# A tower of attention, a selective scan and routed experts for four images: decays of odd late states in SBUF, and another order of the last image's tail

## What is computed

```
h = prelu(((gamma * (q @ k.T)) @ v) @ Wo + bo)            # retention, gamma is 1024 x 1024
x_conv = silu(x_main @ W_conv + b_conv)                    # 128 channels
dt = softplus(x_conv @ W_dt + b_dt);  B, C = x_conv @ W_bc
for s in range(16):                                        # 16 states of 128 channels
    h_s[t] = exp(dt[t] * A[:, s]) * h_s[t-1] + dt[t] * x_conv[t] * B[t, s]
    y[t] += h_s[t] * C[t, s]
out1 = layernorm(h + (y * silu(x_gate)) @ W_out + b_out)
f = relu(out1 @ Wi.T + bi)
for l in range(2):                                         # 64 tokens share one routed expert of 16
    f = relu(shared_l(f) + expert_l(f) + f)
out = layernorm(out1 + f @ Wo.T + bo)
```

## Time and profile before

| | us |
|---|---|
| median of 3 runs (351.4 to 352.4) | 352.08 |
| the profiled execution's own time | 354.25 |
| its span, first to last instruction | 351.9 |
| busy: PE 280.4, DVE 262.4, POOL 259.5, ACT 191.0 | |
| mean granted TensorE clock, share of full speed | 0.902 |

### The profile page before, as it was taken

One profiled execution on the slowest core, in us unless ns is written; L12 is line 12 of the kernel. 1 busy time (PEld: TensorE's weight loads), 2 busy tenths in 40 slices (PEclk: granted clock), 3 DMA queues, 4 the chain that ended last, 5 costly groups with the idle time before them and its releaser, 6 DMA issues.

```text
span 351.9 us, 4676 instructions
## 1 busy us (share of the span) xinstructions
PE 280.4 (80%) x1426; PEld 160.4 (46%) x1426; DVE 262.4 (75%) x287; ACT 191.0 (54%) x298; POOL 259.5 (74%) x136
## 2 busy tenths in 40 slices
PE   8998838784965889998895999977647846887996
PEld 5423402332453343465632434756434535636664
DVE  2466669989778989987989899879988766249420
ACT  2105823337895243689674337893785843357532
POOL 1027067998999999999999799899978889349300
PEclk9999959998789899999999899987976995588999
DMA  7960596766699997776999877678999999536200
GB/s 234 417 258 0 160 313 225 236 249 257 226 306 304 278 394 270 240 277 193 325 307 374 284 239 235 244 233 278 321 304 313 296 309 340 163 122 177 45 2 15
DMA packets 47128, 85.88 MB, mean 244 GB/s; under 512 B 7936, under 2 KB 24832, under 8 KB 46848
## 3 DMA queue, kind: packets, MB, share of 16 engines
q1 hardware_dynamic: 46704, 84.43, 72.8%
q10 hardware_dynamic: 400, 1.17, 1.1%
HBM read 75.62 MB, written 1.57 MB: 219 GB/s over the span
## 4 chain that ended last, share of the span: by engine, by line
PE 24%; DVE 13%; ACT 9%; DMA 6%; issue 4%; POOL 3%; SPq 2%; DVEq 0%; POOLq 0%; ACTq 0%
DVE h L1331 9%; PE acc_y L661 5%; PE tail L720 4%; DMA c_row<-bc_dram 4%; POOL ub L1191 2%; PE acc_r L614 2%; DMA b_row<-bc_dram 2%; PE work L603 2%; DVE decay L1303 2%; ACT decay L915 1%; PE work L752 1%; POOL hc L1202 1%; PE decay L537 1%; ACT decay_own L915 1%; ACT decay L942 1%
## 5 line engine op out<-in xcount | busy, mean ns | idle before, releaser
L1202 POOL TENSOR_TENSOR hc<-h,c_row 128x1024 f32<-128x1024 f32 (+1 forms) x79 | 154.3, 1961 | 30.0 <-DVE h L1331 24.4
L1191 POOL TENSOR_TENSOR ub<-u,b_row 128x1024 f32<-128x1024 f32 (+1 forms) x49 | 98.1, 2003 | 17.2 <-DVE u L1377 11.6
L661 PEld LDWEIGHTS acc_y<-pack,hc 128*128 128x128 f32 x512 | 63.8, 154 | 48.7 <-issue 34.7
L661 PE MATMUL acc_y<-pack,hc 128*128 128x128 f32 x512 | 78.2, 298 | 9.4 <-ACT y_t L1025 4.9
L915 ACT ACTIVATE decay<-delta,neg_a 128x512 f32<-128x512 f32 (+1 forms) x64 | 51.3, 812 | 62.7 <-DVE h L1331 62.1
L1331 DVE TENSOR_TENSOR_SCAN h<-decay,ub 128x512 f32<-128x512 f32 (+1 forms) x41 | 66.0, 1609 | 12.4 <-POOL ub L1191 6.4
L603 PE MATMUL work<-q,kT 64*128 64x512 f32 x112 | 33.7, 679 | 18.4 <-DVE mixed L1357 14.1
L942 ACT ACTIVATE decay<-u 128x512 f32<-128x512 f32 (+1 forms) x42 | 26.5, 640 | 30.4 <-DVE h L1331 30.2
L1303 DVE TENSOR_TENSOR decay<-decay,b_row 128x512 f32<-128x512 f32 (+1 forms) x40 | 30.8, 769 | 14.4 <-DMA b_row<-bc_dram 8.6
L1357 DVE TENSOR_TENSOR mixed<-gam,work 128x512 f32<-128x512 f32 x56 | 35.5, 676 | 7.9 <-PE work L603 7.1
L614 PE MATMUL acc_r<-mixed,v_sb 128*64 128x512 f32 x128 | 36.9, 657 | 1.1 <-DVE mixed L1357 1.0
(11 more groups left out here) (206 smaller groups left out, 347.0 us busy)
## 6 DMA issues: line engine op xcount, KB each, us to landing
b_row<-bc_dram SPq DMA_DIRECT2D x64, 512.0 KB, 5.3
c_row<-bc_dram SPq DMA_DIRECT2D x64, 512.0 KB, 5.9
group_w<-expert_w SPq DMA_DIRECT2D x48, 128.0 KB, 5.0
gam<-gammaT SPq DMA_DIRECT2D x8, 512.0 KB, 10.6
expert_w<-routed_w SPq DMA_DIRECT2D x1, 2048.0 KB, 18.4
gam<-expert_w SPq DMA_DIRECT2D x16, 128.0 KB, 4.7
x_in<-xT SPq DMA_DIRECT2D x4, 256.0 KB, 9.0
pack<-packed ACTq DMA_DIRECT2D x1, 788.0 KB, 6.7
```

The source lines that it names most:

```text
L661: mm = nc.tensor.matmul(acc_y[:, to:to + P], hc[:, at:at + P], ident, start=(job.state == 0 and c % 4 == 0), stop=(job.state == STATES - 1 ...
L1191: nc.gpsimd.tensor_tensor(ub[:, ring(made, job.halves)], u[:, job.image % 2, tokens(q)], b_row[:, ring(job.at, job.halves)], ALU.mult).the ...
L1202: nc.gpsimd.tensor_tensor(hc[:, here], h[:, here], c_row[:, here], ALU.mult).then_inc(hc_ready, job.halves)
```

## The change

Six edits in one:

1. State 12 of images 0 to 2 joins `VECTOR_JOBS`.
2. `KEPT_JOBS`: the vector jobs, and states 7, 9, 11, 13 and 15 of images 0 to 2, have their decays in decay_own (SBUF). `SLOT_JOBS` are the jobs that use slot: all but these odd states. A scan of an odd late state thus reads decay_own and ub.
3. No scan is cut in two any more (`halved` is gone), and no fill of slot either.
4. decay_own grows to 2T, ub shrinks to 2T.
5. In image 3: one late expert load a step over 16 steps in place of two over 8; one dummy matmul of 256 columns (`keep_warm`) in each half step from 2 to 19.
6. The tail of image 2 goes over half steps 2 to 30 (2 + 8 * m // 5), and the eviction of y on ACT moves from half step 19 to 20.

```diff
 VECTOR_JOBS = [q for q, job in enumerate(JOBS)
-               if job.state in ((0, 4, 8, 10, 14) if job.image not in SPLIT else range(0, STATES, 2))]
+               if job.state in ((0, 4, 8, 10, 12, 14) if job.image not in SPLIT else range(0, STATES, 2))]
+KEPT_JOBS = [q for q, job in enumerate(JOBS)
+             if q in VECTOR_JOBS or job.image not in SPLIT and job.state in (7, 9, 11, 13, 15)]
+SLOT_JOBS = [q for q in range(len(JOBS)) if q in VECTOR_JOBS or q not in KEPT_JOBS]
...
-HALF_ACT = {19: "y", 22: "square1", 23: "log1", 24: "f", 26: "layer1", 28: "layer2", 29: "square2", 30: "log2", 31: "rows"}
+HALF_ACT = {20: "y", 22: "square1", 23: "log1", 24: "f", 26: "layer1", 28: "layer2", 29: "square2", 30: "log2", 31: "rows"}
...
+WARM_FROM, WARM_TO = 2, 20
...
-        ub = sb("ub", [P, 3 * T])
-        decay_own = sb("decay_own", [P, T])
+        ub = sb("ub", [P, 2 * T])
+        decay_own = sb("decay_own", [P, 2 * T])
...
-                steps += [(p - 1, m) for m in range(LAST_STEPS) if 2 + 3 * m // 2 == 2 * n + i]
+                steps += [(p - 1, m) for m in range(LAST_STEPS) if 2 + 8 * m // 5 == 2 * n + i]
...
-        def halved(q):
-
-            return JOBS[q].halves == 2 and JOBS[q].state >= TILES - 1
+        def kept_made(q):
+
+            return sum(JOBS[s].halves for s in KEPT_JOBS if s < q)
+
+        def slot_left(q):
+
+            used = [s for s in SLOT_JOBS if s < q and (JOBS[q].halves == 2 or JOBS[s].halves == 2
+                                                       or JOBS[s].at % 2 == JOBS[q].at % 2)]
+            return end_of(used[-1]) if used else 0
...
-                    if p == ALONE and n < TILES:
-                        for g in (2 * n, 2 * n + 1):
-                            look_up_group(p, g)
-                            load_late_group(g)
+                    if p == ALONE:
+                        look_up_group(p, n)
+                        load_late_group(n)
...
+                        if p == ALONE and WARM_FROM <= 2 * n + i < WARM_TO:
+
+                            keep_warm(work[:, HALF:T], 1)
                         for q in ended(start - 4, end - 4):
                             states_out(q)
...
             def own_decay(q):
 
-                made, halves = vector_made(q), JOBS[q].halves
-                if made >= 2:
-
-                    act.wait_ge(scan_done, end_of(job_with(vector_made, VECTOR_JOBS, made + halves - 3)))
-                decay_exp(q, decay_own[:, two_banks(made, halves)], tokens(q))
+                made, halves = kept_made(q), JOBS[q].halves
+                if made + halves > 4:
+
+                    act.wait_ge(scan_done, end_of(job_with(kept_made, KEPT_JOBS, made + halves - 5)))
+                decay_exp(q, decay_own[:, two_rows(made, halves)], tokens(q))
...
-                in_halves = job.halves == 2 and q > 0 and halved(q - 1)
...
+                if slot_left(q):
+                    act.wait_ge(scan_done, slot_left(q))
+                if on_vector(q):
+                    nc.scalar.activation(slot[:, two_banks(job.at, job.halves)], u[:, job.image % 2, tokens(q)], ACT.Copy)\
+                        .then_inc(u_copied, job.halves)
+                else:
+                    decay_exp(q, slot[:, two_banks(job.at, job.halves)], tokens(q))
...
             def scan_job(q):
...
+                here, end = two_banks(job.at, job.halves), end_of(q)
...
+                dve.wait_ge(decay_ready, end)
+                factor = decay_own[:, two_rows(kept_made(q), job.halves)] if q in KEPT_JOBS else slot[:, here]
...
+                nc.vector.tensor_tensor_scan(h[:, ring(job.at, job.halves)], factor, term, initial, ALU.mult, ALU.add)\
+                    .then_inc(scan_done, job.halves)
```

More of the change, by code:

```diff
@@ L933, in fill_slot @@
                     act.wait_ge(next_read, 3)
-                in_halves = job.halves == 2 and q > 0 and halved(q - 1)
-                for at, halves in ((job.at, 1), (job.at + 1, 1)) if in_halves else ((job.at, job.halves),):
-                    if at + halves > 2:
-                        act.wait_ge(scan_done, at + halves - 2)
-                    first = job.first + (at - job.at) * HALF
-                    columns = slice(first, first + halves * HALF)
-                    if on_vector(q):
-                        nc.scalar.activation(slot[:, two_banks(at, halves)], u[:, job.image % 2, columns], ACT.Copy)\
-                            .then_inc(u_copied, halves)
-                    else:
-                        decay_exp(q, slot[:, two_banks(at, halves)], columns)
+                if slot_left(q):
[5 more added lines that the diff above has]
+                    decay_exp(q, slot[:, two_banks(job.at, job.halves)], tokens(q))
             def save_carry(q):
@@ L1141, in _ @@
                         for q in range(len(JOBS)):
-                            if own_limit(start) <= JOBS[q].at < own_limit(end) and on_vector(q):
+                            if own_limit(start) <= JOBS[q].at < own_limit(end) and q in KEPT_JOBS:
                                 own_decay(q)
@@ L1187, in drive @@
                 pool.wait_ge(b_loaded[k % 3], 16 * (k // 3 + 1))
[L1188 to L1191 removed]
+                if made + job.halves > 4:
+                    pool.wait_ge(scan_done, end_of(job_with(gpsimd_made, GPSIMD_JOBS, made + job.halves - 5)))
+                nc.gpsimd.tensor_tensor(ub[:, two_rows(made, job.halves)], u[:, job.image % 2, tokens(q)],
                                         b_row[:, ring(job.at, job.halves)], ALU.mult).then_inc(ub_ready, job.halves)
@@ new lines, in scan_job @@
+                here, end = two_banks(job.at, job.halves), end_of(q)
+                if on_vector(q):
+                    drive(q, here, ring(job.at, job.halves), vector_made(q) + job.halves)
+                    term = slot[:, here]
+                else:
+                    dve.wait_ge(ub_ready, gpsimd_made(q) + job.halves)
+                    term = ub[:, two_rows(gpsimd_made(q), job.halves)]
+                dve.wait_ge(decay_ready, end)
+                factor = decay_own[:, two_rows(kept_made(q), job.halves)] if q in KEPT_JOBS else slot[:, here]
@@ new lines, in scan_job @@
+                if end > 6:
+                    dve.wait_ge(hc_ready, end - 6)
+                    old = JOBS[JOB_OF[end - 7]]
+                    if old.halves == 1 and old.first == 0:
+                        dve.wait_ge(carry_saved, old.state + 1)
+                initial = 0.0
+                if job.first:
+                    dve.wait_ge(carry_saved, job.state + 1)
+                    initial = carry[:, job.state:job.state + 1]
+                nc.vector.tensor_tensor_scan(h[:, ring(job.at, job.halves)], factor, term, initial, ALU.mult, ALU.add)\
+                    .then_inc(scan_done, job.halves)
```

32 lines of the change are left out of this document (4 added, 28 removed).

## The result

| | before | change | ratio [95% interval] |
|---|---|---|---|
| median, us | 352.24 (351.4 to 353.5) | 360.1 (360.05 to 365.3) | 1.026 [1.016, 1.035] |
| span of the profiled execution, us | 351.9 | 357.9 | |

The change makes the kernel 7.9 us slower by the medians (5.8 between the two profiled executions, 354.25 and 360.05). The forecast was 343.2; the third rival, with 360.9, is what happened. Runs were made on several chips, so ratios to the kernel before, run beside each, compare them better than medians.

The account below looks back on a forecast made before the run. Images 0 to 2 were taken as bound by POOL and DVE, image 3 by transfers, then a chain PE, ACT, DVE. Terms -3.4 - 9.1 + 3.6 = -8.9 gave 343.2 us, its own range 338 to 349, overall 334 to 361.

Parts of the forecast that it names:

- the third rival: Late parts, images 0 to 2: odd-state scans and POOL shut each other out for a scan's length; 360.9 us, chance 0.25.
- The same states, POOL: Late states, images 0 to 2: each two-SBUF-input scan costs POOL 0.9 us, taking back DVE's saving; + 3.6 us in three images.
- Late states, DVE: Late states of images 0 to 2: joined scans and drives, less state 12's drive, save DVE 2.1 us an image.
- ACT at state 12: Images 0 to 2: state 12's two preparations stand behind softplus on ACT; 1.3 us lost, leaving DVE some 0.8 an image.
- The rings don't bind: Late states of images 0 to 2: two places in ub do what three did, so the smaller ring costs nothing.
- Image 3, first half: Transfers set its pace; eight expert loads moved to the second half save 3.4 us (1.5 to 5).
- Image 3, second half: Later tail matrices and full clock shorten DVE's waits for y (to 1.9 us) and norm (to 2.2); 9.1 us saved.
- The dummies: Image 3: eighteen dummy matmuls take PE 10 us, hidden in its idle time, and the clock mostly stays at 2.4 GHz.

Follow-up runs that it names:

- pool_halves: The change with POOL's C products of states 6, 8, 10, 12 and 14 of images 0 to 2 cut in two: 356.4 us, ratio 1.018.
- odd_slot_12pool: The change with decays of states 7, 9, 11, 13, 15 back in slot, whole, and state 12's drive back on POOL: 349.1 us, ratio 0.996.
- odd_in_slot: The change with decays of states 7, 9, 11, 13, 15 of images 0 to 2 back in slot (PSUM), whole: 357.8 us, ratio 1.018.
- image3_rings_12: The kernel before with image 3's edits, the change's decay_own and ub sizes, halving kept, state 12's drive on DVE: 350.8 us, ratio 1.002.
- image3_only_2: The same program as image3_only, run again on the chip of image3_rings_12: 344.1 us, ratio 0.983.
- image3_rings: image3_only with the change's two buffer sizes, decay_own grown to 2T and ub shrunk to 2T: 343.1 us, ratio 0.975.
- no_spread_loads: image3_only with two expert loads a step, as in the kernel before, in place of one: 351.2 us, ratio 0.997.
- no_dummies: image3_only without the dummy matmuls: 346.1 us, ratio 0.984.
- image3_only: The kernel before with only the edits of image 3 (one load a step, dummy matmuls, tail to half step 30): 344.5 us, ratio 0.981.
- old_tail: image3_only with the tail over 28 half steps as before and ACT's y part a half step earlier: 345.9 us, ratio 0.982.

## Why the prediction was wrong

Two steps failed. **The one that set the length of the change's late parts** is headed "The same states, POOL": "I price it by columns fetched, 0.9 us, since that is the row's own number for that many columns." The row was u's, in which DVE came first and POOL lost 0.83 us. Two things were wrong in carrying it over. The price goes by the holder's time, not by its columns: a scan holds on for all its 2.1 us, as the second pieces of pool_halves show (2.0 us lost). And which side loses was read as a property of the engines ("DVE itself has lost nothing beside POOL in any row"), where it is one of order. u happened to come first; the odd scans come 0.1 to 1.3 us behind a C product. At 160.38 the reason can be read: the scan waits for its ub, made by POOL, and POOL goes on from ub to the C product without a gap (157.92, 160.24), 0.14 us before DVE starts. So DVE lost 2.1 us a scan and POOL then waited 2.28 for h. Measured was 2.1 us of DVE's time a scan, and 11.4 us of idle POOL in the late part of image 1, where the prediction had 5 x 0.9 of POOL's time and 1.2 of waiting. Stated as the third rival, this gave 45.7 us for the late part; measured are 44.7, 44.5 and 42.9. That 360.9 came within 1 us of the median has some luck in it: its images 0 to 2 are 2.8 us too long and its image 3 is 0.8 too short, while the medians lie 1.8 us further apart than the spans. The chance of 0.25 for it was too low: the only row on the question showed a nearly full stop.

The rule of the Trainium skill (SBUF — State Buffer, section "Who interferes with whom") weighed there, that the two exclude each other for a whole instruction and that order decides who loses, agrees with this trace: 2.02 + 2.14 us at 151.31. Its sum, 17.7 us above mine, would have been 360.9.

**The other is "Late states, DVE"**, "2.1 us less an image": not seen. A whole scan takes 2.29 and the halving is gone, as said, but the step counted only DVE's instructions. With whole scans the fill of slot for the next state can't run behind a first piece: DVE waits for fills for 26.1 us in odd_slot_12pool, 6.8 with halves. That run shows + 1.7 us an image where this term, without state 12's drive, would be 3.4 less. In the change most of these fills are gone with the odd decays, and the exclusion takes their place. So the exclusion isn't the whole of the miss: with the decays back in slot the late parts are still 42.0 us.

**ACT at state 12**, a loss of 1.3 beside 1.3 of drive, 2.6 in all: mechanism and size were right. odd_in_slot against odd_slot_12pool (late parts) and image3_rings_12 against image3_only_2 (medians) put the two together at 2.4 and 2.2 us an image. What was wrong is what stood against them: the 2.3 us of POOL that the drive gives back are true of its busy time and worth nothing.

**The rings don't bind**: nothing speaks against it (image3_rings, 343.1 against 344.5).

**Image 3, first half**, - 3.4, at most 5: measured - 5.5, a little more than the 5.2 that I had worked out as all that can come. POOL is busy for the whole of it, 28.70 us. Its cause, the loads, is shown by no_spread_loads (35.3 us). The clock added to it, 2.4 us in no_dummies, which I had not counted in this half. The slower images ahead of it did not: image3_only, without them, has 29.2 us for the change's 29.3.

**Image 3, second half**, - 9.1: measured - 6.2. The y wait (1.7 for 1.9) and the norm wait (2.5 for 2.2) came as worked out, 9.5 us together. The term failed by what was not in it: moving the tail to later half steps makes the matrices late for ln_y, where DVE waits 4.7 us (old_tail has no such wait). A wait of 3.4 us for b_row, in the same half of the kernel before, went, and kept the total from being worse.

**The dummies** took 12.3 us for 10, hidden: without them the kernel is no faster. That the clock "mostly stays" held in the change, 0.96 in the second half; that the dummies are the reason in that half is not shown: no_dummies had the matrices back at 1.9 us, and image3_only_2 had one at 3.51 us in spite of dummies.

In sum the image 3 terms were 12.5 and came to 11.7; that of images 0 to 2 was + 3.6 and came to + 18.5. On the ladder above, 5.2 of the latter come from whole scans and fills, 7.2 from state 12 and 6.1 from the decays in SBUF, as edits made in this order. In another order the shares would differ. How long a late part with the odd decays in SBUF would be without the exclusion, no run shows.

## What to carry to other kernels

Before moving an operand from PSUM to SBUF, look at what GpSimd does at that moment: in these traces a VectorE instruction with both inputs in SBUF and a GpSimd product took the sum of their times, and the one that started a moment later lost. One row on a collision gives its mechanism, not its price for another pair: ask who holds, for how long, and who will be second. And joining halves into wholes saves issue time on one engine while it takes the overlap from the engine that refills: here 1.7 us an image lost, with VectorE's instructions 3.4 us shorter by the count above. Last, see whether a stage bound by transfers starts with some of them done: a slower stage ahead of it can make it look better.

## What was not expected of the hardware

- Which engine loses is decided within 0.14 us: at 160.24 POOL started, at 160.38 DVE, and DVE waited for 2.22 us. The waiting shows as a longer instruction, not as idle time: DVE's busy share rose from 75% to 80% in a slower kernel.
- The same program took 39.5 and 45.1 us for image 3's second half in two executions (image3_only, 344.5 us, and image3_only_2, 349.2 us), with a granted clock of 0.96 and 0.81. So a single trace of this kernel is uncertain by more than most of the effects looked for.
